# Patch embedding of a vision tower: seven of eight block products for seven pairs of chunks

## The chip, the cores and the metric

The kernel runs on one core of a Trainium2 chip. The metric is the device time of one execution in microseconds (us). Three runs of the kernel before took 1721.77, 1724.46 and 1727.43 us, so its median is 1724.46 us. One further execution was taken by the hardware profiler, and all rows below come from it.

## The reference

128 images of 3 x 224 x 224 fp32 pass through a patch embedding and two transformer layers (attention, a routed MLP, attention, a mixture of two of eight experts). Only the first step is touched by the change:

```
patches = X.reshape(B, 3, 8, 28, 8, 28).transpose(0, 2, 4, 1, 3, 5).reshape(B, 64, 2352)
tokens  = einsum('bpi,hi->bph', patches, W) + b          # 2352 -> 128
tokens  = concatenate([class_token, tokens], axis=1) * pos_embed
```

It is one matrix product: 128 outputs, a contraction over 2352 = 18 x 128 + 48 inputs, and 128 x 64 = 8192 patches as columns, all in fp32.

## The kernel before, in words

The program is a chain of stages, each a block in which the five engines run their own instruction lists and meet at its end. `patch_embed` (L100) is the first; `layer_norm`, `attention` and the rest follow and read `h`, the tokens that `patch_embed` writes.

The patches are cut into 16 chunks of 8 images, that is 512 columns each. The host lays a chunk out as 18 slices of 128 inputs (`x_main`, 4.6 MB a chunk) and a rest of 48 inputs (`x_tail`). The buffer `xb` holds two whole chunks of 18 slices.

- SyncE (`block.sync`) issues all loads of x on one queue. Chunk c is loaded in six transfers of 768 KB (three slices each, L168) once chunk c-2 has been used; for the first chunk each is preceded by the three weight slices of the same place (L167). The rests of two chunks follow (L181), one in partitions 0 to 47 and one in 64 to 111 of `xe`.
- TensorE (`block.tensor`) takes two chunks at a time. For each it accumulates 18 matmuls of a 128x128 weight slice with a 128x512 slice of x in one PSUM bank (L201). Then come the two matmuls of the rests (L209), with 64 rows each. An fp32 matmul appears in the trace as two MATMUL records and two LDWEIGHTS records.
- VectorE adds the bias, multiplies by the position embedding and writes `h` (L228), one instruction a chunk.
- ScalarE waits for the fourth chunk and then loads the constants of the later stages (L131); GpSimd prepares a few small constants from them. Both are nearly idle in this stage.

The loops are written with `pipelined`, which puts the middle of the work into a hardware loop. The stage ends for the others when TensorE's last product is done and VectorE has written the last two chunks; the next stage's first matmul (L329) needs that.

The functions below are those that the diff touches, with what calls them.

Of the kernel before, what the change touches and what calls it, by code (L numbers as in the profile page):

```python
# [14 lines left out]
ALU = mybir.AluOpType  # L15
ACT = mybir.ActivationFunctionType
# [26 lines left out]
class At:  # L43


    def __init__(self, index, slot):
        self.index, self.slot = index, slot


def pipelined(eng, items, unroll, depth, lag, step):  # L50

    groups, lead = items // unroll, -(-(depth + lag) // unroll)
    assert lead < groups

    def group(g, fixed):
        for j in range(unroll):
            def at(s, j=j):  # L60
                slot = (j - s) % unroll
                if fixed:
                    i = g * unroll + j - s
                    return At(i, slot) if 0 <= i < items else None
                return At(g * unroll + (j - s), slot)
            step(j, at)

    for g in range(lead):
        group(g, True)
    with eng.Fori(lead, groups) as g:  # L70
        group(g, False)
    for g in range(groups, -(-(items + depth) // unroll)):
        group(g, True)


# [24 lines left out]
def patch_embed(nc, images, x_main, x_tail, h, ps, w_src, w_tok, b_tok, pos, cls, own_loads, later_loads, consts):  # L100

    n = CHUNK_IMAGES * PATCHES
    chunks = images // CHUNK_IMAGES
    pieces = 6
    kp = KT // pieces
    half = P // 2
    ctx, sb, sem = stage_scope(nc)  # L110
    with ctx:  # L111
        xb = sb("x_chunk", [P, 2, KT, n])
        xe = sb("x_ends", [P, 2, n])
        x_in = [[sem(f"x_in_{s}_{i}") for i in range(pieces)] for s in range(2)]
        end_in = [sem(f"x_end_in_{s}") for s in range(2)]
        w_in = [sem(f"w_in_{i}") for i in range(pieces)]
        w_end_in, ends_clear = sem("w_end_in"), sem("ends_clear")
        x_used, tok_ps = sem("x_used"), sem("tok_ps")
        tok_done, cls_done = sem("tok_done"), sem("cls_done")
        own_loaded, later_loaded = sem("own_loaded"), sem("later_loaded")  # L120
        means_set, gelu_done, asum_done, folded = sem("means_set"), sem("alphas_gelu"), sem("alpha_summed"), sem("folded")
        block = ctx.enter_context(nc.Block())

        @block.scalar
        def _(act):
            for dst, src in own_loads:
                act.dma_start(dst, src).then_inc(own_loaded, 16)
            act.wait_ge(own_loaded, 16 * len(own_loads))
            act.wait_ge(tok_ps, 4)
            for dst, src in later_loads:  # L130
                act.dma_start(dst, src).then_inc(later_loaded, 16)  # L131
            act.wait_ge(later_loaded, 16 * len(later_loads))
            nc.scalar.activation(consts.alphas[:, :, :], consts.alpha_raw, ACT.Gelu).then_inc(gelu_done, 1)
            act.wait_ge(gelu_done, 1)

        @block.gpsimd
        def _(pool):
            nc.gpsimd.memset(consts.mean_w[:, :], 1.0 / D).then_inc(means_set, 1)
            nc.gpsimd.memset(consts.spread_w[:, :], 1.0 / 32).then_inc(folded, 1)
            nc.gpsimd.memset(consts.dist_pair[:, :, :], 0.0).then_inc(folded, 1)  # L140
            pool.wait_ge(means_set, 1)
            pool.wait_ge(later_loaded, 16 * len(later_loads))
            nc.gpsimd.tensor_tensor(consts.center_w[:, :], consts.ident[:, :], consts.mean_w[:, :], ALU.subtract)\
                .then_inc(folded, 1)
            nc.gpsimd.tensor_scalar(consts.neg_b_q[:, :], consts.b_q, -1.0, None, ALU.mult).then_inc(folded, 1)
            pool.wait_ge(gelu_done, 1)
            nc.gpsimd.tensor_tensor(consts.asum[:, :], consts.alphas[:, :, 0], consts.alphas[:, :, 1], ALU.add)\
                .then_inc(asum_done, 1)
            pool.wait_ge(asum_done, 1)
            nc.gpsimd.tensor_tensor(consts.asum[:, :], consts.asum[:, :], consts.alphas[:, :, 2], ALU.add)\  # L150
                .then_inc(asum_done, 1)
            pool.wait_ge(asum_done, 2)
            nc.gpsimd.tensor_tensor(consts.abv[:, :], consts.asum[:, :], consts.bv_col, ALU.mult).then_inc(folded, 1)
            pool.wait_ge(folded, 5)

        @block.sync
        def _(sp):
            def step(j, at):
                a = at(0)
                s = a.slot % 2  # L160
                fixed = isinstance(a.index, int)
                if not (fixed and a.index < 2):
                    sp.wait_ge(x_used, a.index - 1)
                for i in range(pieces):
                    ks = slice(i * kp, (i + 1) * kp)
                    if fixed and a.index == 0:
                        sp.dma_start(w_tok[:, ks, :], w_src[:, ks, :]).then_inc(w_in[i], 16)  # L167
# [19 lines left out]
        def _(pe):  # L187
            def step(j, at):
# [3 lines left out]
                if not (fixed and a.index < 2):  # L192
                    pe.wait_ge(tok_done, a.index * 2 - 2)
# [2285 lines left out]
```

## Time and profile before

| | us |
|---|---|
| median of three runs | 1724.46 |
| lowest, highest | 1721.77, 1727.43 |
| span of the profiled execution | 1699.7 |
| first matmul of the patch embedding | 6.47 |
| its last matmul record begins and lasts | 265.39, 1.13 for the last four |
| first matmul of the next stage | 268.45 |
| TensorE busy over the whole span | 1616.2 (95%) |
| VectorE, ScalarE, GpSimd busy | 1082.2, 869.2, 782.4 |

The span runs from the first to the last instruction; the runs are timed around the whole execution, which adds some 25 us. PE is TensorE, PEld its weight loads, DVE is VectorE, ACT is ScalarE, POOL is GpSimd, SP is SyncE; a q behind the name is the engine's sequencer or queue. A row of the lines view gives source line, engine, operation, output <- inputs, shapes, count, then busy time and mean ns of one, then the idle time of the engine ahead of the group and what ended it. A row of the windows view gives, for one stretch of time, its length and each engine's busy time with the number of instructions, then the granted TensorE clock, the share of time the DMA engines were busy and what they moved in GB/s. The patch embedding is the first 268 us of the span.

### The profile page before, as it was taken

How to read it: one execution, taken by the hardware profiler on the slowest of the kernel's cores; microseconds unless marked ns; L12 is line 12 of the kernel's file. 1: busy time of each engine (PE TensorE's matmuls, PEld its weight loads, DVE VectorE, ACT ScalarE, POOL GpSimd, SP SyncE). 2: the span in 40 equal slices, each digit the busy share in tenths (PEclk: the TensorE clock that was granted, in tenths of full speed). 3: DMA queues.
4: the chain of work that ended last, by engine and by line, in shares of the span. 5: the costliest groups of instructions: out<-in, count | busy, mean ns of one | idle time of the engine just before them, and what ended most of it. 6: DMA issues, size and time to landing. Idle time of an engine off the chain costs nothing. (4 is left out here: it accounts for less than half of the span.)

```text
span 1699.7 us, 61682 instructions
## 1 busy us (share of the span) xinstructions
PE 1616.2 (95%) x24097; PEld 1203.3 (71%) x24097; DVE 1082.2 (64%) x3361; ACT 869.2 (51%) x2334; POOL 782.4 (46%) x932
## 2 busy tenths in 40 slices
PE   8999999899999999997989998999999999869997
PEld 3444444677877777776567755888888888659997
DVE  0000005688888888885676664577777777768875
ACT  0000004666666666663544445566766666547753
POOL 0000000588888888886001111445555555645554
PEclk9999999999999999999989999999999999969999
DMA  9887860000000000000400000000000000135431
GB/s 366 338 309 301 321 244 1 2 4 4 3 3 3 3 3 3 3 3 4 111 1 1 1 1 5 3 8 22 22 21 21 21 24 18 36 102 154 141 80 44
DMA packets 47214, 117.17 MB, mean 69 GB/s; under 512 B 10731, under 2 KB 29470, under 8 KB 46972
## 3 DMA queue, kind: packets, MB, share of 16 engines
q1 hardware_dynamic: 39198, 99.25, 16.4%
q0 software_dynamic: 6096, 12.94, 2.2%
q8 instruction: 191, 3.13, 0.8%
q10 hardware_dynamic: 1678, 1.43, 0.3%
q14 instruction: 51, 0.42, 0.1%
HBM read 96.80 MB, written 18.61 MB: 68 GB/s over the span
## 5 line engine op out<-in xcount | busy, mean ns | idle before, releaser
L1545 PE MATMUL ps<-xn,s_a_wqkv 128*128 128x260 f32 x1024 | 276.9, 402 | 4.5 <-DMA s_a_wqkv<-in_f_b 2.9
L201 PE MATMUL ps<-x_chunk,s_w_tok 128*128 128x512 f32 x576 | 252.1, 599 | 6.5 <-DMA x_chunk<-in_x_main 6.5
L201 PEld LDWEIGHTS ps<-x_chunk,s_w_tok 128*128 128x128 f32 x576 | 109.9, 192 | 147.4 <-issue 147.4
L1545 PEld LDWEIGHTS ps<-xn,s_a_wqkv 128*128 128x128 f32 x1024 | 177.0, 191 | 50.2 <-issue 16.3
L228 DVE SCALAR_TENSOR_TENSOR h<-ps,s_b_tok,s_pos 128x512 f32 (+1 forms) x16 | 11.3, 746 | 248.8 <-PE ps L209 248.8
L886 POOL TENSOR_TENSOR prob_a<-e_a,inv_sum_a 128x512 f32<-128x512 f32 x64 | 66.9, 1045 | 194.4 <-issue 113.4
L2161 POOL DMA_INDIRECT out<-h,xn x93 | 97.6, 1049 | 89.6 <-DVE h L2276 85.1
L1629 PE MATMUL ps<-s_a_wqkv,xn_pair_a 128*64 128x256 f32 x1024 | 138.8, 391 | 0.0
L941 ACT ACTIVATE resT_a<-ps 128x260 f32<-128x260 f32 x256 | 85.2, 386 | 101.4 <-PE ps L1596 64.6
L1411 DVE TENSOR_REDUCE neg_max_a<-ps 128x8 f32<-128x520 f32 x128 | 89.2, 697 | 70.8 <-PE ps L1519 48.5
L870 POOL TENSOR_TENSOR kept_a<-e_a,keep_a 128x585 f32<-128x585 f32 x64 | 87.2, 1362 | 71.0 <-issue 60.4
L1596 PE MATMUL ps<-probT_a,horner_a 64*64 64x65 f32 x2048 | 113.6, 228 | 4.2 <-issue 2.6
L771 POOL MEMSET cls_queries_a<- 128x1040 f32 x2 | 1.9, 966 | 238.1 <-POOLq L283 238.1
L1586 PE MATMUL ps<-dv_a,probT_a 64*64 64x64 f32 x2048 | 107.0, 223 | 2.8 <-DVE probT_a L1170 2.3
L1586 PE MATMUL ps<-horner_a,probT_a 64*64 64x64 f32 x2048 | 105.7, 220 | 0.6 <-issue 0.6
L929 ACT ACTIVATE qk_a<-ps 128x260 f32<-128x260 f32 x256 | 96.4, 387 | 18.7 <-PE ps L1545 11.8
L1586 PEld LDWEIGHTS ps<-dv_a,probT_a 64*64 64x64 f32 x2048 | 82.3, 136 | 27.5 <-issue 27.4
L2051 POOL TENSOR_TENSOR h<-h,mlp_gated 128x320 f32<-128x320 f32 x26 | 22.4, 860 | 167.8 <-DVE mlp_gated L2031 167.8
L394 ACT ACT_TABLE_LOAD x3 | 3.8, 1283 | 184.1 <-PEq L111 176.8
L1596 PE MATMUL ps<-probT_a,cls_values_a 64*64 64x1 f32 x2048 | 91.6, 187 | 3.3 <-issue 3.2
L1420 DVE TENSOR_TENSOR e_a<-ps,neg_max_a 128x520 f32<-128x520 f32 x128 | 89.7, 701 | 6.0
L1106 ACT ACTIVATE e_a<-e_a 128x585 f32<-128x585 f32 (+1 forms) x128 | 85.3, 666 | 14.7 <-DVE e_a L1420 7.7
(280 smaller groups left out, 4265.6 us busy)
## 6 DMA issues: line engine op xcount, KB each, us to landing
x_chunk<-in_x_main SPq DMA_DIRECT2D x96, 768.0 KB, 8.8
xn<-pair_rows SPq DMA_DIRECT2D x93, 130.0 KB, 2.1
pair_rows<-pad_rows_m SPq DMA_DIRECT2D x29, 130.0 KB
s_f_all<-in_f_w SPq DMA_DIRECT2D x2, 1024.0 KB
x_ends<-in_x_tail SPq DMA_DIRECT2D x16, 96.0 KB, 10.8
out<-h,xn POOLq DMA_INDIRECT x93
s_w_tok<-in_w_tok SPq DMA_DIRECT2D x6, 192.0 KB, 8.2
pair_rows<-rows_m,slot_i_m POOLq DMA_INDIRECT x65, 2.5
```

The source lines that it names most:

```text
L201: last = nc.tensor.matmul(ps[:, bank, :], w_tok[:, k, :], xb[:, s, k, :], start=(k == 0), stop=False)
L870: nc.gpsimd.tensor_tensor(columns(kept, t.even), columns(e_of(t), t.even), columns(keep, t.even), ALU.mult).then_inc(kept_done, 1)
L929: nc.scalar.activation(qk[:, (t.j // 2) % 2, c, :], ps[:, QK_BANK[i], 0:QUAD], ACT.Identity if bias is not None else ACT.Copy, bias=bias[: ...
L941: nc.scalar.activation(res_t[:, k // 2, :, at[0], at[1], :], ps[:, R_BANK[i], 0:CH * SEQ].rearrange("p (c q) -> p c q", q=SEQ), ACT.Copy). ...
L1106: nc.scalar.activation(columns(e_of(t), t.even), columns(e_of(t), t.even), ACT.Exp, scale=-SCALE)\
L1411: last = nc.vector.tensor_reduce(neg_max[:, :, 0:CH], score(), AX.X, ALU.min)
L1420: last = nc.vector.tensor_tensor(e_of(t)[:, :, 0:CH], score(), over_keys(neg_max[:, :, 0:CH]), ALU.subtract)
L1545: nc.tensor.matmul(ps[:, QK_BANK[i], 0:QUAD], w_qkv[:, c * P:(c + 1) * P], xn[:, t.h * QUAD:(t.h + 1) * QUAD], start=True, stop=True).then ...
L1586: last = nc.tensor.matmul(ps[rows, 2 + n, col:col + DH], pt[rows, k, c, i, 1:SEQ], values[rows, i, c, :], start=True, stop=True)
L1596: last = nc.tensor.matmul(ps[other, R_BANK[i], c * SEQ:c * SEQ + cols], values[rows, (t.j - 6) % 2, i, c, :], pt[rows, k, c, i, 0:cols], s ...
L1629: last = nc.tensor.matmul(ps[b * DH:(b + 1) * DH, V_BANK, i * CH * DH:(i + 1) * CH * DH] .rearrange("p (c d) -> p c d", c=CH), xs[:, k, i ...
L2161: nc.gpsimd.indirect_dma_start(self.out[:, :], bass.IndirectOffsetOnAxis(ap=blk[:, s % RB, self.NAME:self.NAME + 1].bitcast(mybir.dt.int32 ...
```

## The change

The chunks are taken in eight pairs and the 18 slices as nine pairs (slice k with slice k+9; HK = 9). In a step k the four 64-column halves of the two weight slices and the four x slices (two chunks, two slices) form a 2 x 2 block product. Before, it took four 128-column matmuls, which are eight products of a 64-column half. Strassen's method (in Winograd's form) does it with seven, from sums and differences of the blocks, and adds the seven results up afterwards. Seven pairs of chunks (63 steps) are done this way and the eighth the former way.

- TensorE does seven matmuls a step with 64 weight columns, each writing one half (partitions 0 to 63, `lo`, or 64 to 127, `hi`) of one of four PSUM banks. The order within a step begins with `lo` in even steps and with `hi` in odd ones, so that the halves alternate over the whole stream. Pairs of chunks alternate between banks 0 to 3 and 4 to 7.
- VectorE computes for each step three differences of 128x512 slices (`tr[.., 0]`, `[.., 1]`, `[.., 3]`), staggered over three iterations: iteration j makes term 0 of step j, term 1 of step j-1 and term 3 of step j-2. GpSimd computes the fourth difference (`tr[.., 2]`). The ring `tr` has four places and lies in `xn`, which is free in this stage.
- VectorE also forms the five weight sums, once for each three slices.
- After nine steps ScalarE copies the four banks to SBUF with eight instructions (`evict`), GpSimd adds parts with five instructions (`join` at its k = 5), VectorE adds two more and finishes the two chunks (`join` at its k = 8).
- x is loaded in sets of three steps (12 transfers of 256 KB for the first set, one step at a time; 4 transfers of 768 KB for a later one) into three buffers; set s waits for the steps of set s-3. The tail of the second chunk is loaded once more (`xd`), and GpSimd makes a difference of the tails.
- ScalarE loads the constants of the later stages behind its first eviction. The hardware loops of the stage are gone: all is unrolled.

The core of the diff (the removed code is printed above):

```diff
+    folded = pairs - 1
+    HK = KT // 2
+    TRI = 3
+    SETS = HK // TRI
+    steps = folded * HK
+    RT = 4
...
+        xb = sb("x_chunk", [P, SETS, 4, TRI, n])
+        sums = sb("w_sums", [P, 5, HK, half])
+        tr = xn[:, 0:RT * 4 * n].rearrange("p (r q n) -> p r q n", r=RT, q=4)
...
+            for s in range(pairs * SETS):                                   # SyncE
+                p, i = divmod(s, SETS)
+                if s < SETS:
+                    load_w(i)
+                    load_w(SETS + i)
+                since(sp, step_done, TRI * (s - SETS + 1))
+                for kk in range(TRI if s == 0 else 1):
+                    for q in range(4):
+                        c, k = 2 * p + q % 2, (q // 2) * HK + i * TRI
+                        if s == 0:
+                            load(xb[:, 0, q, kk:kk + 1, :], c, k + kk, 1).then_inc(first_in[kk], 16)
+                        else:
+                            load(xb[:, i, q, :, :], c, k, TRI).then_inc(x_in[i], 16)
...
+                t = tr[:, m % RT]                                           # TensorE, step m
+                sides = ((0, lo), (1, hi)) if low_first else ((1, hi), (0, lo))
+                for i, side in sides:
+                    product(0, side, w_tok[:, (HK + k, k)[i], lo], x_at(m, (2, 0)[i]))
+                pe.wait_ge(t_done[0], m + 1)
+                pe.wait_ge(t_done[1], m + 1)
+                for i, side in sides:
+                    product(2, side, sums[:, i, k, :], t[:, i])
+                pe.wait_ge(t_done[3], m + 1)
+                for i, side in sides:
+                    product(1, side, sums[:, 3 + i, k, :], (x_at(m, 3), t[:, 3])[i])
+                pe.wait_ge(t_done[2], m + 1)
+                product(3, lo if low_first else hi, sums[:, 2, k, :], t[:, 2], start=k < 2, stop=k >= HK - 2)\
+                    .then_inc(step_done, 1)
...
+            def third_term(m):                                              # GpSimd
+                x_ready(pool, m)
+                since(pool, step_done, m - RT + 1)
+                nc.gpsimd.tensor_tensor(tr[:, m % RT, 2], x_at(m, 3), x_at(m, 1), ALU.subtract)\
+                    .then_inc(t_done[2], 1)
...
+            for j in range(steps + 2):                                      # VectorE
+                if j < steps:
+                    if j < HK and j % TRI == 0:
+                        weight_sums(j // TRI)
+                    x_ready(dve, j)
+                    since(dve, step_done, j - RT + 1)
+                    nc.vector.tensor_tensor(tr[:, j % RT, 0], x_at(j, 1), x_at(j, 0), ALU.subtract)
+                if 1 <= j <= steps:
+                    dve.wait_ge(t_done[0], j)
+                    nc.vector.tensor_tensor(tr[:, (j - 1) % RT, 1], x_at(j - 1, 3), tr[:, (j - 1) % RT, 0], ...)
+                if j >= 2:
+                    dve.wait_ge(t_done[1], j - 1)
+                    nc.vector.tensor_tensor(tr[:, (j - 2) % RT, 3], tr[:, (j - 2) % RT, 1], x_at(j - 2, 2), ...)
+                p, k = divmod(j, HK)
+                if k == 8 and p and j < steps:
+                    join(p - 1)
+            join(folded - 1)
```

## Rows read from the trace of the kernel before

**Rows 1.** Windows of the patch embedding, and of the start of the next stage.
```profile
0.00:10.00 10.00, 3.53 (x4) 1.51 (x5) 1.25 (x2) 0.00 (x0) 0.70 (x7) 1.00 0.72 244
10.00:30.00 20.00, 20.00 (x46) 8.89 (x45) 0.00 (x0) 0.00 (x0) 0.00 (x0) 1.00 1.03 396
100.00:200.00 100.00, 100.00 (x237) 43.22 (x236) 4.23 (x6) 0.00 (x0) 0.00 (x0) 1.00 0.77 301
270.00:300.00 30.00, 27.86 (x219) 13.26 (x217) 21.97 (x33) 16.07 (x30) 0.53 (x1) 1.00 0.01 2
```

**Rows 2.** Lines of 0 to 255 us: who waits in the stage.
```profile
L201 PE MATMUL ps<-x_chunk,s_w_tok 128*128 128x512 f32 x552 | 241.8, 599 | 6.5 <-DMA x_chunk<-in_x_main 6.5
L228 DVE SCALAR_TENSOR_TENSOR h<-ps,s_b_tok,s_pos 128x512 f32 x10 | 7.0, 746 | 153.9 <-PE ps L209 153.9
```

**Rows 3.** Timeline of TensorE: start us, us, engine line, what, how many records.
```profile
6.47 6.00 PE L201 MATMUL ps<-x_chunk,s_w_tok 128*128 128x512 f32 x7 [6.47 <-DMA x_chunk<-in_x_main]
...
40.30 1.13 PE L209 MATMUL ps<-x_ends,s_w_tok 64*128 64x512 f32 x4
41.36 8.85 PE L201 MATMUL ps<-x_chunk,s_w_tok 128*128 128x512 f32 x20
...
265.39 1.13 PE L209 MATMUL ps<-x_ends,s_w_tok 64*128 64x512 f32 x4
266.72 1.41 DVE L228 SCALAR_TENSOR_TENSOR h<-ps,s_b_tok,s_pos 128x512 f32 x2 [30.75 <-PE ps L209]
```

**Rows 4.** Timeline of TensorE in attention, full width and half width.
```profile
699.71 2.20 PE L1545 MATMUL ps<-xn,s_a_wqkv 128*128 128x260 f32 x8
704.66 1.08 PE L1629 MATMUL ps<-s_a_wqkv,xn_pair_a 128*64 128x256 f32 x8
```

**Rows 5.** Timeline: a VectorE stream beside a GpSimd instruction, one input in PSUM.
```profile
700.62 1.28 DVE L1157 TENSOR_TENSOR horner_a<-ps,v_alpha_a 128x512 f32<-128x512 f32 x2
700.83 1.43 POOL L870 TENSOR_TENSOR kept_a<-e_a,keep_a 128x585 f32<-128x585 f32 x1 [1.33 <-issue]
```

**Rows 6.** One source line of VectorE each: count, ns min/median/max; its two inputs are in SBUF.
```profile
L1306 DVE TENSOR_TENSOR weight_of_choice_m<-each_choice_m,choice_weights_m x16: 224/1061/1120, 1115.5 to 1491.9; 128x64 f32<-128x64 f32 x15, 128x80 f32<-128x80 f32 x1
```

**Rows 7.** Timeline around one of them.
```profile
1252.10 0.22 DVE L1300 TENSOR_TENSOR each_choice_m<-s_expert_ids,index_m 128x64 f32<-128x64 f32 x1
1252.35 1.12 DVE L1306 TENSOR_TENSOR weight_of_choice_m<-each_choice_m,choice_weights_m 128x64 f32<-128x64 f32 x1
...
1252.34 1.04 POOL L886 TENSOR_TENSOR prob_a<-e_a,inv_sum_a 128x512 f32<-128x512 f32 x1 [3.62 <-DVE inv_sum_a L1455]
```

**Rows 8.** One source line each: ns min/median/max of the nearest GpSimd, VectorE, ScalarE instructions.
```profile
L855 POOL TENSOR_TENSOR cls_values_a<-dv_a,horner_a x64: 1261/1272/1281, 329.0 to 797.3; 128x512 f32<-128x512 f32 x64
L886 POOL TENSOR_TENSOR prob_a<-kept_a,inv_sum_a x64: 1040/1042/1047, 313.6 to 786.2; 128x512 f32<-128x512 f32 x64
L1157 DVE TENSOR_TENSOR horner_a<-ps,v_alpha_a x128: 678/680/692, 324.6 to 800.2; 128x512 f32<-128x512 f32 x128
L1993 DVE TENSOR_TENSOR first_choice<-s_expert_ids,index_r x13: 491/493/494, 861.7 to 983.9; 128x320 f32<-128x320 f32 x13
L966 ACT ACTIVATE v_raw_a<-ps x64: 597/598/605, 307.9 to 781.5; 128x512 f32<-128x512 f32 x64
```

**Rows 9.** Windows with the granted clock behind stretches of little TensorE work.
```profile
310.00:315.00 5.00, 1.71 (x40) 1.04 (x40) 3.32 (x9) 3.23 (x11) 2.83 (x4) 1.00 0.00 0
315.00:320.00 5.00, 4.86 (x48) 3.86 (x48) 2.87 (x11) 3.21 (x9) 4.47 (x5) 0.66 0.00 0
325.00:330.00 5.00, 4.18 (x108) 3.40 (x108) 3.94 (x13) 3.04 (x9) 4.83 (x6) 1.00 0.01 3
```

**Rows 10.** DMA issues of the stage: KB each, median us from issue to landing.
```profile
x_chunk<-in_x_main SPq DMA_DIRECT2D x96, 768.0 KB, 8.8
```

More of the change, by code:

```diff
@@ L40 @@
 ROW = 2 * D + 4
[L43 to L73, printed above, removed]
 spent = []
@@ L134, in _ @@
             act.wait_ge(gelu_done, 1)
+            for p in range(2, folded):
+                evict(p)
         @block.gpsimd
         def _(pool):
-            nc.gpsimd.memset(consts.mean_w[:, :], 1.0 / D).then_inc(means_set, 1)
[L139 to L142, printed above, removed]
@@ L186, in _ @@
-        @block.tensor
-        def _(pe):
-            def step(j, at):
-                a = at(0)
-                fixed = isinstance(a.index, int)
-                first = fixed and a.index == 0
-                if not (fixed and a.index < 2):
-                    pe.wait_ge(tok_done, a.index * 2 - 2)
-                for s in range(2):
-                    bank = 2 * a.slot + s
-                    for i in range(pieces):
-                        if first and s == 0:
-                            pe.wait_ge(w_in[i], 16)
-                        pe.wait_ge(x_in[s][i], a.index * 16 + 16)
-                        for k in range(i * kp, (i + 1) * kp):
-                            last = nc.tensor.matmul(ps[:, bank, :], w_tok[:, k, :], xb[:, s, k, :],
-                                                    start=(k == 0), stop=False)
-                    last.then_inc(x_used, 1)
-                if first:
-                    pe.wait_ge(w_end_in, 32)
-                pe.wait_ge(end_in[a.slot], (a.index - a.slot) * 16 + 32)
-                for s in range(2):
-                    rows = slice(s * half, (s + 1) * half)
-                    nc.tensor.matmul(ps[:, 2 * a.slot + s, :], w_tok[rows, KT, :], xe[rows, a.slot, :],
-                                     start=False, stop=True).then_inc(tok_ps, 1)
-            pipelined(pe, chunks // 2, 2, 0, 2, step)
@@ new lines, in _ @@
+            nc.gpsimd.memset(consts.mean_w[:, :], 1.0 / D).then_inc(means_set, 1)
+            nc.gpsimd.memset(consts.spread_w[:, :], 1.0 / 32).then_inc(folded_w, 1)
+            nc.gpsimd.memset(consts.dist_pair[:, :, :], 0.0).then_inc(folded_w, 1)
+            for m in range(steps):
+                p, k = divmod(m, HK)
+                third_term(m)
+                if k == 1:
+                    ends_gap(p)
+                if k == 5 and p:
+                    join(p - 1, m)
+                if p == 3 and k == 2:
+                    fold_constants()
@@ L213, in _ @@
+            join(folded - 1, steps - 1)
+            pool.wait_ge(folded_w, 5)
         @block.vector
@@ L236 @@
+            join(folded - 1)
+            for c in range(2):
+                dve.wait_ge(tok_ps, c + 1)
+                finish(2 * folded + c, ps[:, 4 * (folded % 2) + c, :])
 class Router:
```

240 lines of the change are left out of this document (173 added, 67 removed).

## Prediction

> **What bounds the kernel now.** I read the windows of the first stage first. TensorE is busy for every microsecond from 6.47 us on, at full clock, while the DMA share falls to 0.77 in mid-stage [rows 1]: the loads have room, and in the lines no matmul waits for one after the first [rows 2]. VectorE has one instruction a chunk and waits for TensorE, GpSimd and ScalarE have next to nothing. So TensorE's stream sets the length: it runs from 6.47 to 266.5 us, and VectorE's last two instructions follow [rows 3]. In the timeline 20 records take 8.85 us [rows 3]; less the 0.16 us by which a record (0.59 us) outlasts the pace, that is 0.43 us a record, 0.86 us a matmul. 288 matmuls are 248 us; the rests of a pair of chunks add about 1.26 us (1.06 from start to start and two slower changes, eight times, 10 us), and the first records run at half pace (7 in 6.0 us), 2 us more. That is the 260 us seen. All later stages start from `h` and are not touched.
>
> **What TensorE saves.** A step is 8 half-width products before (4 matmuls, 8 records, 3.44 us) and 7 after. This only helps if two half-width products run at once. Attention shows it: 8 records of 128x64 weights on 256 columns, alternating between the two halves, take 1.08 us, while 8 full-width records of 260 columns take 2.20 us one after the other [rows 4]. So the pair costs what one costs, and since the halves alternate across steps the odd seventh product pairs with the first of the next step. A step costs 3.5 x 0.86 = 3.01 us, 63 steps save 63 x 0.43 = 27 us. The rests (now four 64x64 products, one on each quarter) I leave at 1.26 us. The last lone half and the change of width before the last pair give back 0.5 us. TensorE alone would so save 26.6 us.
>
> **What feeds it.** Each step now needs three VectorE differences and one GpSimd difference of 128x512, and a pair of chunks needs in addition on GpSimd five joining sums and one of the tails, on VectorE two sums and two finishing instructions: 31 VectorE and 15 GpSimd instructions in a pair, nearly all with both inputs in SBUF. VectorE's nearest rows are 0.68 us for one with an input in PSUM, two in 1.28 us, so 0.60 us from start to start [rows 5, 8]; 320 columns with both in SBUF take 0.49 us, on the same line of 0.16 us plus one element per 1.04 ns [rows 8]. GpSimd's are 1.27 us with two full inputs and 1.04 us with one broadcast [rows 8]. Taken each by itself: VectorE 31 x 0.60 = 18.6 us, GpSimd 15 x 1.27 = 19 us, TensorE 9 x 3.01 + 1.26 = 28.35 us. Both would hide.
>
> They do not run by themselves. L1306, a VectorE product of 64 columns with both inputs in SBUF, should take 0.22 us as its neighbour L1300 does, and its median is 1.06 us [rows 6, 7]. In the timeline GpSimd's 1.04 us instruction starts at 1252.34 and the VectorE one at 1252.35; it ends 0.09 us after GpSimd's end [rows 7]. It stood still for the whole of it. L1157, with one input in PSUM, runs beside GpSimd at its normal pace [rows 5]. So two-input SBUF work on the two engines adds up instead of overlapping. The Trainium skill, "SBUF — State Buffer", section "Who interferes with whom", says the same as a rule: a VectorE instruction with two SBUF inputs and a GpSimd instruction that reads SBUF exclude each other, and whichever comes second waits until the first is finished. By that rule the change's two streams are one; a rule of free overlap would give the saving above.
>
> The price of a pair of chunks, as one stream: of 31 VectorE instructions 15 follow a GpSimd one; such a one has its start-up hidden (L1306 ends 0.09 us behind, not 0.22), so 0.55 us, the other 16 take 0.60: 17.9 us. 15 GpSimd instructions at 1.23 us (1.27 less a little overlap from start to start): 18.5 us. Together 36.3 us against TensorE's 28.35, so this stream becomes the bound. Its two ends: 31 x 0.55 + 15 x 1.04 = 32.7 us if GpSimd holds VectorE off only for the shorter of its two times, and 31 x 0.69 + 15 x 1.27 = 40.4 us if nothing of a start-up is hidden. I take 36.3, which uses the rows of the same shape. ScalarE's eight copies (0.60 us each, 4.8 us a pair) [rows 8] lie beside all this: the join starts on GpSimd only two steps later.
>
> **The start.** VectorE's iteration j first waits for the x of step j, and then makes the last term of step j-2. So TensorE cannot finish step 1 before the x of step 3 is there, which is set 1, a semaphore that wants all 3.15 MB. Through set 1 the queue moves 0.39 + 3.15 + 0.35 (rests) + 0.39 + 3.15 = 7.4 MB. At 2.44 MB by 10 us and 396 GB/s behind [rows 1] this is 22.6 us, plus 1 us to be signalled, and I add 2 for the first set's short 2 KB rows: 25.5 us (23 to 28). Set 2 follows 3.54 MB, 8.6 us, later at 34. Before, TensorE had been running since 6.47 us.
> From 25.5 us the shared stream goes on: iterations 3 to 8 are 6 x (3 x 0.60 + 1.23) = 18.2 us, the last weight sums some 1.8 us (five of 192 columns at 0.35, an estimate between the 0.22 of 64 columns and 0.49 of 320 [rows 7, 8]), the tail difference 1.2 us: 46.7 us. Set 2 is not late for this (wanted at about 36). Six more pairs, each with the join of the one before: 6 x 36.3 = 218 us, to 264.5. Two iterations and the end of step 62 add 3.5: 268. Then the classic pair, 72 x 0.43 + 0.1 + 1.26 = 32.3 us, beside which the last join (some 14 us) hides: TensorE ends at 300.3 us, where it ended at 266.5. VectorE's two final instructions are the same. The sum is +34 us.
>
> Loads in the steady state: a set of 3.15 MB takes some 2 us to start and 7.9 us to move at 396 GB/s (a single transfer lands in 8.8 us at the median, in a full queue [rows 10]); a pair of 36 us needs three, so they are no bound. SyncE's wait for a used set holds back only the sets and tails behind it. What stands behind VectorE's waits is every later difference, in order; that is why one late set or one GpSimd instruction reaches TensorE. The later stages' constants (1.4 MB, now earlier) fit as well. The stage's sequencers get more instructions; I charge nothing, since attention issues more per microsecond.
>
> **Forecast.** Against the profiled execution's own time the span goes from 1699.7 to about 1734 us; the runs' median lies 24.8 us above that span, for what is around it, so 1724.5 + 34 = 1758 us. With the two ends of the pair's price (6 x -3.6 and 6 x +4.1 us, pair 0 with them by -2 to +3) and of the start (2.5 us either way) this case spans 1732 to 1788.
>
> **Rivals.**
> (1) No exclusion that matters: the engines' long instructions interleave after all, or GpSimd's are blocked for only a small part. Then TensorE binds. Step 1's last term comes at 25.5 + 1.9 = 27.4; the rest of step 1 and step 2 at half pace, after the long idle time, end at 33.5; six steps and the rests 19.3: pair 0 done at 52.8. Six pairs at 28.35 are 170, the lone half and change 0.5, the classic pair 32.2: 255.6 us, 11 less than 266.5; with 2 us lost once to the constants' transfer, -9: 1715 us. For it: each engine's own busy sum fits. Against it: with a median of 1.06 us at least half of L1306's 16 instances were held off. The time turns from a loss to a gain when a pair costs less than about 31 us.
> (2) TensorE's clock falls. With 28 us of work in 36 it stands still for about 1 us in a step. Behind 1.71 us of work in 5 us the granted clock was 0.66 in the next window, but with 4.18 of 5 it stayed at 1.00 [rows 9]. If it ran at 1.2 GHz throughout, a step would take 6.0 us and 54 steps about 108 us more than the 4.0 of the forecast: 1865 us. Gaps of 1 us speak against it.
> (3) The halves don't pair at 512 columns, so that the change does not do what it says: 7 x 0.86 = 6.0 us a step, 63 x 2.6 = 162 us more, about 1890 us with the start. Rows 4 speak against it; I know of no row at 512 columns.
>
> **How the numbers follow.** The forecast 0.77, rival 1 0.14, rival 2 0.06, rival 3 0.03. 0.3% (5 us) is about what a measurement of this kernel tells from no change. Rival 1's spread reaches into that band, as does the lowest end of the forecast's: faster 0.12, within 0.05, slower 0.83. The range 1722 to 1792 leaves out most of rival 1 and all of rivals 2 and 3.
>
> **What would show it.** In the new profile VectorE's differences with a mean well over 0.69 us, near 1.1, or GpSimd's over 1.27; in a mid-stage window the two engines' own work summing to the whole time while TensorE is at some 75%; TensorE idle before the third to sixth product of a step and released by VectorE's terms; a pair period of 36 us. If the periods are 28 us and the differences 0.69 us, the exclusion is what I had wrong. The start is right if step 1 waits until about 27 us. The half-width products should show 7 in 3.0 us where nothing waits.

## The result, and the profile after

| | before | after |
|---|---|---|
| median of four runs, us | 1724.99 | 1769.51 |
| lowest, highest | 1721.77, 1727.43 | 1768.43, 1771.34 |
| span of the profiled execution | 1699.7 | 1768.1 |
| first matmul of the next stage | 268.45 | 307.32 |
| VectorE, GpSimd busy over the span | 1082.2, 782.4 | 1310.9, 951.3 |

The change makes the kernel slower by 44.5 us: ratio 1.026, with the 95% interval 1.0244 to 1.0276. The forecast was 1758, its range 1722 to 1792. The patch embedding itself ends 38.9 us later, where +34 was forecast.

The profiled spans differ by 68.4 us, which is more than the runs show. The one profiled execution of before was a short one: in a second one of the same kernel (e5 below) the span is 1725.1 us, the next stage starts at 268.39 us, as before, and 17 of the 25.4 us between the two lie in the second attention stage, which the change doesn't touch. So medians are compared with medians here, and of the profiled executions only the stage.

Windows of the kernel after, as in [rows 1]: stretch, its length, then busy time and count of TensorE, its weight loads, VectorE, ScalarE and GpSimd, then granted clock, DMA share, GB/s.

```profile
0.00:10.00 10.00, 0.88 (x2) 0.29 (x4) 4.03 (x8) 0.00 (x0) 1.54 (x8) 1.00 0.79 244
10.00:30.00 20.00, 9.94 (x24) 2.32 (x22) 12.02 (x14) 0.00 (x0) 9.23 (x6) 0.92 1.04 382
24.00:34.00 10.00, 4.46 (x13) 1.39 (x14) 6.50 (x8) 0.00 (x0) 4.07 (x3) 0.66 0.85 345
...
100.00:200.00 100.00, 83.66 (x356) 24.70 (x354) 96.14 (x84) 9.51 (x16) 69.74 (x47) 0.97 0.72 271
...
260.00:300.00 40.00, 38.53 (x116) 15.47 (x113) 11.58 (x16) 4.75 (x8) 8.58 (x7) 1.00 0.44 163
```

In the hundred microseconds in which TensorE had been busy throughout [rows 1] it is now busy for 83.66. VectorE shows 96.14 for 84 instructions and GpSimd 69.74 for 47. Together that is more than 100, because a blocked instruction counts as busy on its own engine while the other one works. The DMA share is 0.72: the loads have room.

The lines of 0 to 320 us show the same from the waiter's side. Columns as in [rows 2].

```profile
L167 PE MATMUL ps<-xn,w_sums 128*64 128x512 f32 x504 | 194.6, 622 | 26.5 <-DVE xn L351 23.3 <-DVE xn L347 3.2
L249 POOL TENSOR_TENSOR xn<-x_chunk 128x512 f32<-128x512 f32 x63 | 102.6, 1638 | 90.3 <-PE ps L167 72.3 <-DMA x_chunk<-in_x_main 17.5
...
L347 DVE TENSOR_TENSOR xn<-x_chunk,xn 128x512 f32<-128x512 f32 x63 | 82.2, 1305 | 0.0
L343 DVE TENSOR_TENSOR xn<-x_chunk 128x512 f32<-128x512 f32 x63 | 72.3, 1147 | 23.2 <-DMA x_chunk<-in_x_main 12.7 <-PE ps L167 10.0
...
L351 DVE TENSOR_TENSOR xn<-xn,x_chunk 128x512 f32<-128x512 f32 x63 | 66.9, 1063 | 0.0
```

VectorE's three differences take 1.31, 1.15 and 1.06 us in the mean, where a free one takes 0.68; TensorE's idle time ends on two of them. The same three, and GpSimd's difference, by source line: ns min/median/max.

```profile
L343 DVE TENSOR_TENSOR xn<-x_chunk x63: 677/693/1797, 9.1 to 262.7; 128x512 f32<-128x512 f32 x63
...
L347 DVE TENSOR_TENSOR xn<-x_chunk,xn x63: 677/1750/1805, 12.4 to 267.1; 128x512 f32<-128x512 f32 x63
...
L249 POOL TENSOR_TENSOR xn<-x_chunk x63: 1283/1729/1876, 9.2 to 260.5; 128x512 f32<-128x512 f32 x63
```

There are two kinds of each and little between them: a VectorE instruction takes 0.68 us when it is free and about 1.75 when it comes second, and GpSimd's takes 1.28 or about 1.73. In the timeline one can see them stand on each other (start us, duration us, engine, line):

```profile
156.72 1.71 POOL L254 TENSOR_TENSOR x_ends_gap<-x_ends,x_ends_gap 64x512 f32<-64x512 f32 x1
...
157.23 1.75 DVE L343 TENSOR_TENSOR xn<-x_chunk 128x512 f32<-128x512 f32 x1
158.90 0.68 DVE L347 TENSOR_TENSOR xn<-x_chunk,xn 128x512 f32<-128x512 f32 x1
159.50 0.68 DVE L351 TENSOR_TENSOR xn<-xn,x_chunk 128x512 f32<-128x512 f32 x1
...
160.24 1.11 PE L167 MATMUL ps<-x_chunk,w_sums 128*64 128x512 f32 x1 [3.21 <-DVE xn L351]
```

GpSimd's tail difference runs to 158.43. VectorE's L343, begun at 157.23, ends 0.55 us behind it; the next two, with GpSimd idle, take 0.68. TensorE stands for 3.21 us until the third of them. Its first records behind such a gap take 1.11 us instead of 0.59: the granted clock is 0.66 in the window of 24 to 34 us, which mixes the levels of 1.2 and 2.4 GHz, and 0.50, the lower level throughout, from 29.6 to 33.0 us, right behind the first gap.

### The profile page after: what moved, and what is told of

Its sections match the earlier page's. It is cut to its first block and busy times, and to the rows that moved or that the text cites. A ratio compares the mean times of both kernels' runs of the same rounds, so it can differ in the third digit from the quotient of the medians.

```text
span 1768.1 us, 62873 instructions
## 1 busy us (share of the span) xinstructions
PE 1630.3 (92%) x24503; PEld 1183.1 (67%) x24503; DVE 1310.9 (74%) x3580; ACT 904.1 (51%) x2391; POOL 951.3 (54%) x1037
## 5 line engine op out<-in xcount | busy, mean ns | idle before, releaser
L167 PE MATMUL ps<-xn,w_sums 128*64 128x512 f32 x504 | 194.6, 622 | 26.5 <-DVE xn L351 23.3
L249 POOL TENSOR_TENSOR xn<-x_chunk 128x512 f32<-128x512 f32 x63 | 102.6, 1638 | 90.3 <-PE ps L167 72.3
L167 PEld LDWEIGHTS ps<-xn,w_sums 128*64 128x64 f32 x504 | 56.1, 142 | 111.1 <-issue 73.1
L167 PE MATMUL ps<-x_chunk,s_w_tok 128*64 128x512 f32 x252 | 99.9, 625 | 9.1 <-DMA x_chunk<-in_x_main 9.1
L1649 PE MATMUL ps<-qk_a 64*64 64x65 f32 x4096 | 95.8, 225 | 12.0 <-issue 10.8
L1649 PEld LDWEIGHTS ps<-qk_a 64*64 64x64 f32 x4096 | 76.2, 134 | 41.2 <-issue 34.3
L229 ACT ACTIVATE part_a<-ps 128x512 f32<-128x512 f32 x7 | 4.2, 598 | 183.5 <-PE ps L167 183.5
```

Source lines behind the costliest of these rows:

```text
L167: return nc.tensor.matmul(ps[side, base + bank, :], weights, moving, start=k == 0 if start is None else start, stop=k == HK - 1 if stop is ...
L249: nc.gpsimd.tensor_tensor(tr[:, m % RT, 2], x_at(m, 3), x_at(m, 1), ALU.subtract)\
L1649: last = nc.tensor.matmul(ps[i * PATCHES:(i + 1) * PATCHES, b, c * SEQ:(c + 1) * SEQ], qk[rows, sl, c, t0 + 1:t0 + SEQ], qk[rows, sl, CH + ...
```

## The experiments

**e1: the two engines side by side, measured alone.** The kernel before with spare 128x512 instructions at the start of VectorE and GpSimd, in six phases, while TensorE does its usual work.

```diff
+            for phase, behind in enumerate((10, 10, 17, 24, 31)):
+                pool.wait_ge(m_pool, 2 + 5 * phase)
+                pool.wait_ge(m_dve, behind)
+                for r in range(5):
+                    if phase == 3:
+                        nc.gpsimd.memset(u[11 + r], 0.5).then_inc(m_pool, 1)
+                    else:
+                        nc.gpsimd.tensor_tensor(u[11 + r], u[9], u[10], ALU.add).then_inc(m_pool, 1)
...
+            for phase, behind in enumerate((2, 7, 12, 17, 22)):
...
+                for r in range(7):
+                    if phase == 4:
+                        last = nc.vector.tensor_copy(u[2 + r], u[0])
+                    elif phase == 2:
+                        last = nc.vector.tensor_tensor(u[2 + r], ps[:, 6, :], u[1], ALU.add)
+                    else:
+                        last = nc.vector.tensor_tensor(u[2 + r], u[0], u[1], ALU.add)
```

> The kernel before, with 35 VectorE and 25 GpSimd instructions of 128x512 fp32 on spare data added to the patch embedding, where both engines are idle. Phases of 7 and 5: VectorE alone; GpSimd alone; both with two SBUF inputs; VectorE with one input in PSUM beside GpSimd with two in SBUF; VectorE with two SBUF inputs beside a GpSimd memset; a VectorE copy beside GpSimd with two SBUF inputs. Exclusion theory: alone 0.60 us from start to start and 1.27 us; together the phase lasts as long as the sum, 7 x 0.6 + 5 x 1.2 = 10.2 us; with a PSUM input and beside the memset both run as alone (the longer of 4.2 and 6.3 us). Rival, that the two only share bandwidth or that VectorE was slowed by TensorE and the loads: together about 6.5 us, or VectorE already slow when alone.

Windows of e1, one for each phase: VectorE alone; GpSimd alone; both with two SBUF inputs; VectorE with one input in PSUM beside GpSimd; VectorE beside GpSimd's memset; VectorE's copy (one input) beside GpSimd.

```profile
7.83:12.13 4.30, 4.30 (x8) 1.75 (x7) 4.30 (x7) 0.00 (x0) 0.00 (x0) 1.00 1.02 416
12.29:18.48 6.19, 6.19 (x15) 2.66 (x14) 0.00 (x0) 0.00 (x0) 6.14 (x5) 1.00 1.02 407
18.53:28.21 9.68, 9.68 (x24) 4.33 (x23) 9.68 (x7) 0.00 (x0) 7.93 (x5) 1.00 1.03 377
28.25:34.55 6.30, 6.30 (x16) 2.84 (x15) 4.27 (x7) 0.00 (x0) 6.19 (x5) 1.00 1.02 417
34.61:38.95 4.34, 4.34 (x11) 1.90 (x10) 4.30 (x7) 0.00 (x0) 2.38 (x5) 1.00 1.01 415
38.99:46.78 7.79, 7.79 (x20) 3.07 (x19) 7.79 (x7) 0.00 (x0) 7.06 (x5) 1.00 1.03 366
```

Seven VectorE instructions alone take 4.30 us (0.614 each), five of GpSimd 6.19 (1.238 each). Side by side they take 9.68, where full overlap would give 6.19 and a plain sum 10.49. With one VectorE input in PSUM both run as if alone (4.27 and 6.19), and beside a memset too (4.30). So whether the two exclude each other goes by where the inputs lie, and nothing of it comes from this stage's waits: TensorE is busy throughout at full clock in all six phases, and the one run took 1724.76 us. The Trainium skill, "SBUF — State Buffer", section "Who interferes with whom", states these cases as a rule, the harmless write-only GpSimd instruction among them; all phases agree with it.

**e2: the change, with GpSimd reading nothing in its difference.** A memset of the same tile stands in its place, so the fourth difference is left out of the result.

```diff
-                nc.gpsimd.tensor_tensor(tr[:, m % RT, 2], x_at(m, 3), x_at(m, 1), ALU.subtract)\
-                    .then_inc(t_done[2], 1)
+                nc.gpsimd.memset(tr[:, m % RT, 2], 0.5).then_inc(t_done[2], 1)
```

> The changed kernel, with GpSimd's difference of each step replaced by a memset of the same tile (that term is left out of the result). Exclusion theory: GpSimd reads SBUF only in six instructions a pair, 31 x 0.60 + 6 x 1.23 = 26 us, under TensorE's 28.4; the pair falls from 35.9 to about 28.7 us, 6 x 7.2 = 43 us and some 4 us of the first pair: near 1723 us. Rival, that VectorE is slowed by TensorE's streams or by the loads: the pair stays at 35 to 36 us and half of VectorE's differences at 1.75 us.

1725.02 us against 1723.10, ratio 1.0013 (0.9991 to 1.0035); the next stage starts at 267.57 and a pair of chunks takes (217.0 - 36.6) / 6 = 30.1 us. Lines of e2, 0 to 300 us:

```profile
L350 DVE TENSOR_TENSOR xn<-xn,x_chunk 128x512 f32<-128x512 f32 x63 | 57.9, 921 | 0.0
...
L346 DVE TENSOR_TENSOR xn<-x_chunk,xn 128x512 f32<-128x512 f32 x63 | 51.6, 819 | 0.0
...
L249 POOL MEMSET xn<- 128x512 f32 x63 | 32.5, 525 | 118.2 <-PE ps L167 67.7 <-DMA x_chunk<-in_x_main 50.1
```

With one instruction of GpSimd a step no longer reading SBUF, +1.9 us is left of +44.5, though the waits, semaphores and transfers are the same. The instruction is also 0.7 us shorter, and e2 alone doesn't tell which of the two counts: if the memset still excluded VectorE, a pair would be 31 x 0.614 + 6 x 1.238 + 9 x 0.53 = 31.2 us, near the 30.1 measured; e1's fifth phase tells it. GpSimd's six other instructions a pair still block, as the means of 0.92 and 0.82 us show. They were in my expectation of 28.7 us, though, and don't explain the 1.4 us over it. Most of that lies in the second pair: from VectorE's first difference (L342) of this pair to that of the next it is 35.3 us, 4.8 of them VectorE's waits for x, and from then on 29.1, 28.6, 29.9 and 29.7 us.

**e3: the joining sums moved from GpSimd to VectorE,** spread over five iterations.

```diff
-                if k == 5 and p:
-                    join(p - 1, m)
...
+                if part == 0:
+                    dve.wait_ge(evicted, 8 * (p + 1))
+                    add(part_d[hi, 0, :], part_d[hi, 0, :], part_d[hi, 1, :])
+                    add(swap_c[:, :], swap_c[:, :], part_c[:, :])
```

> The changed kernel, with the five joining sums of a pair moved from GpSimd to VectorE and spread over its iterations; GpSimd keeps the fourth difference and that of the tails. Exclusion theory: 36 x 0.60 + 10 x 1.2 = 33.6 us a pair instead of 35.9, so 6 x 2.3 = 14 us less than the changed kernel, near 1756 us. Rival, that each engine is slow by itself: VectorE has five more instructions at its present mean of 1.17 us, 6 us a pair more, near 1800 us.

1749.15 against 1723.10, ratio 1.0153 (1.0128 to 1.0178); pair (240.4 - 38.4) / 6 = 33.7 us; next stage at 293.16, 14.2 us earlier than after the change, where 14 was expected. The median less its own before fell by 18.5.

**e4: GpSimd's whole share on VectorE.** Added to e3: the fourth difference and that of the tails.

```diff
-                third_term(m)
...
+                if 1 <= j <= steps:
+                    nc.vector.tensor_tensor(tr[:, (j - 1) % RT, 2], x_at(j - 1, 3), x_at(j - 1, 1),
+                                            ALU.subtract).then_inc(t_done[2], 1)
```

> The changed kernel with everything on VectorE: four differences a step, the tails' difference and the joining sums; GpSimd has nothing to do but the small constants. Exclusion theory: 46 x 0.60 = 27.6 us a pair, just under TensorE's 28.4; the pair takes 28.5 to 30 us, some 40 us less than the changed kernel, 1722 to 1738 us. Rival, that VectorE's instructions are slow by themselves here: 46 x 1.17 = 54 us a pair, about 110 us more than the changed kernel.

1722.61 against 1723.10, ratio 0.9998 (0.9981 to 1.0016); pair (214.0 - 36.9) / 6 = 29.5 us; next stage at 265.13. Lines of e4, 0 to 300 us:

```profile
L340 DVE TENSOR_TENSOR xn<-x_chunk 128x512 f32<-128x512 f32 x63 | 43.2, 686 | 22.8 <-DMA x_chunk<-in_x_main 19.0 <-PE ps L167 3.6
...
L344 DVE TENSOR_TENSOR xn<-x_chunk,xn 128x512 f32<-128x512 f32 x63 | 43.0, 683 | 0.0
```

This is the opposite of what one does by busy sums: 46 instructions on one engine are faster by 6.4 us a pair than 31 and 15 on two. A GpSimd instruction costs the shared stream 1.24 us, the same work on VectorE 0.61. The window of e4, 100 to 200 us, has both engines near full:

```profile
100.00:200.00 100.00, 99.95 (x463) 41.98 (x461) 98.61 (x160) 14.28 (x24) 0.00 (x0) 1.00 0.88 335
```

**e5: the kernel before, once more,** unchanged, to see whether its first profiled span was ordinary.

> The kernel before, unchanged, profiled once more. Its first profiled execution had a span of 1699.7 us, while its timed runs are 1719 to 1729 us; for the changed kernel time and span differ by 1.7 us only. If the first profiled execution was a fast outlier in the second attention loop (570 us from the first to the last of its value projections, against 586 in every other profile so far), this one shows a span near 1721 us, the patch embedding ending again at 268.4 us and the loop at 586. If the profiler really leaves out 25 us for this kernel, the span is again 1700.

One run of 1726.87 us, with a span of 1725.1: what lies around the span is 1.8 us and not 24.8. The next stage starts where it did. The row of a source line of attention, count and ns as above, then first and last start:

```profile
L1629 PE MATMUL ps<-s_a_wqkv,xn_pair_a x1024: 379/379/431, 306.7 to 1483.2; 128*64 128x256 f32 x171
```

**e6: e4 with a start by single steps.** The first nine steps of x are loaded and awaited one by one instead of by threes, and in each iteration the terms whose data are there come ahead of the one that waits.

```diff
-                for kk in range(TRI if s == 0 else 1):
+                for kk in range(TRI if s < SETS else 1):
...
+                if j < steps:
+                    if j < HK and j % TRI == 0:
+                        weight_sums(j // TRI)
+                    x_ready(dve, j)
```

> Everything on VectorE, and in addition the first nine steps' x loaded and signalled step by step, and within an iteration the third difference ahead of the wait for the next x. Theory: the shared stream being gone, what is left of the loss is the late start (step 1 waits for all of set 1 at 25.5 us); with it cured step 3 ends near 24 instead of 36 us, and the stage about 12 us earlier: 1706 to 1714 us, below the kernel before. Rival, that the start does not matter because VectorE's 46 instructions a pair bind afterwards: within 3 us of the version with the old start, 1720 to 1726 us.

1711.68 against 1722.34, ratio 0.9936 (0.9911 to 0.9961); first rests at 26.4 (e4: 36.9), pair 29.6, next stage at 254.55, 10.6 us earlier than in e4, where some 12 was expected. It is faster than both kernels.

**e7: the start alone.** The change with the loads by single steps, the order of the terms and GpSimd's share as they were.

```diff
-        first_in = [sem(f"x_first_{i}") for i in range(TRI)]
+        first_in = [sem(f"x_first_{i}") for i in range(HK)]
...
-                for kk in range(TRI if s == 0 else 1):
+                for kk in range(TRI if s < SETS else 1):
```

> The changed kernel with only the loads and signals of the first nine steps made step by step; GpSimd keeps its work and VectorE its order. Exclusion theory: the shared stream of 36 us a pair binds from the third step on, but it can begin some 8 us earlier, so up to 8 us less than the changed kernel, 1761 to 1768 us. Rival, that the slow start is the larger part of the loss: 20 us or more are won.

1758.60 against 1722.34, ratio 1.0209 (1.0179 to 1.0240), a little under the 1761 to 1768 that I expected. That the time is near is luck: of up to 8 us expected in this stage it gained 0.65, since the next stage starts at 306.67. Step 3 of pair 0, behind which the first rests stand, is done 7.9 us earlier (31.5 against 39.4), pair 0 itself only 4.1 us (the first eviction begins at 53.45 against 57.59). The timeline of e7 shows the first place where the gain goes: VectorE wants set 3 at 39.5 us and it isn't there yet, while the change comes to it at 48.35 and doesn't wait.

```profile
43.05 0.69 DVE L343 TENSOR_TENSOR xn<-x_chunk 128x512 f32<-128x512 f32 x1 [3.52 <-DMA x_chunk<-in_x_main]
43.09 3.45 POOL L249 TENSOR_TENSOR xn<-x_chunk 128x512 f32<-128x512 f32 x2 [4.97 <-DMA x_chunk<-in_x_main]
```

VectorE's first final sum (L328), once a pair, starts at 76.80, 114.18, 151.60, 189.04, 226.46 and 263.90 in e7 and at 80.88, 116.53, 152.47, 189.71, 227.09 and 264.55 after the change. So 4.1 us are left at the first join, and e7's pairs then take 37.4 us throughout, while the change's took 35.7 and 35.9 before they took 37.2 to 37.5. The windows of the change's first and third of these periods show what the short ones lack:

```profile
80.88:116.53 35.65, 31.48 (x142) 9.57 (x140) 35.28 (x32) 6.25 (x10) 24.17 (x15) 1.00 0.73 276
...
152.47:189.71 37.24, 31.84 (x136) 9.47 (x134) 35.38 (x33) 4.75 (x8) 24.04 (x15) 0.95 0.70 262
```

The granted clock is 1.00 in the change's two short periods and 0.95 in its three long ones and in all five of e7. In the long ones TensorE stands for 3.2 us behind the join, its next records run at half pace, and VectorE's first difference of a later step then waits for TensorE to free a place of the ring: 1.77, 1.93 and 1.98 us, at 163.75, 201.15 and 238.59. In the short ones its waits for TensorE are 0.3 us and 1.2 us in all. So at the joins the low clock does reach the shared stream, by some 1.6 us a pair (an estimate, 37.4 less 35.8). No run here changes the clock alone, and a gap of 3.2 us in the second short period left it at 1.00, so why it falls in one pair and not in the other stays open. That the timed median is 11 us under the change's, with its own reference 2.7 lower, is mostly outside this stage.

**e8: the fourth difference on VectorE, the joins left on GpSimd.** Other half of e4, as e3 is the first.

```diff
-                third_term(m)
...
+                    nc.vector.tensor_tensor(tr[:, (j - 1) % RT, 2], x_at(j - 1, 3), x_at(j - 1, 1),
+                                            ALU.subtract).then_inc(t_done[2], 1)
```

> The changed kernel with the fourth difference moved to VectorE, the joining sums and the tails' difference left on GpSimd. Exclusion theory: 40 x 0.60 + 6 x 1.2 = 31.2 us a pair instead of 35.9, about 28 us for six pairs and some 3 of the first: near 1738 us. It should lie between the version with all on VectorE (1722.6) and that with the joining sums there (1749.2). Rival, that each engine is slow by itself: nine more VectorE instructions of 1.17 us a pair, slower than the changed kernel.

1734.27 against 1722.34, ratio 1.0074 (1.0050 to 1.0099); pair (224.0 - 36.2) / 6 = 31.3 us, where 31.2 was expected; next stage at 274.61.

With e1's prices the four divisions of the same work can be set beside each other; the plain sum is 0.614 us for each VectorE and 1.238 for each GpSimd instruction of a pair:

| | VectorE, GpSimd instructions | plain sum | measured pair | next stage | median less its own before |
|---|---|---|---|---|---|
| the change | 31, 15 | 37.6 | 35.9 | 307.32 | +44.5 |
| e3 | 36, 10 | 34.5 | 33.7 | 293.16 | +26.1 |
| e8 | 40, 6 | 32.0 | 31.3 | 274.61 | +11.9 |
| e4 | 46, 0 | 28.2 | 29.5 | 265.13 | -0.5 |

The measured pair is the mean from the first rests to those of the seventh pair. It follows the plain sum, less 0.7 to 1.7 us, as long as GpSimd has part of it; e4's mean holds waits for x up to 87 us, and its last four periods of L340 are 29.7, 28.6, 29.3 and 28.7 us. By work that overlaps, GpSimd's 18.6 us a pair (15 x 1.238) and VectorE's 19.0 (31 x 0.614) would have hidden behind TensorE, and the change would have run at TensorE's own pace.

**e9: e6 with the later stages' constants loaded after the sixth eviction,** to take their 1.4 MB out of the crowded queue of the start.

```diff
-            evict(0)
+            for p in range(folded - 1):
+                evict(p)
             for dst, src in later_loads:
                 act.dma_start(dst, src).then_inc(later_loaded, 16)
-            evict(1)
+            evict(folded - 1)
```

> The version with everything on VectorE and the stepwise start, in addition with the loads of the later stages' constants (1.4 MB) moved from behind the first eviction to behind the sixth, where the queue of x has room. If these loads hold back x in the second pair, the stage ends up to 3.5 us earlier (1.4 MB at 0.4 MB per us). If not, nothing changes: TensorE's long wait in that version is at 41 to 47 us, before they are issued at 52, so I expect no more than 1 us and 1710 to 1713 us.

1713.76 against 1727.70, ratio 0.9922 (0.9903 to 0.9942); next stage at 254.10 against e6's 254.55. Nothing to speak of, as expected.

**e10: e9 with twelve steps by single loads** in place of nine. In e6 TensorE waits at 41 to 47 us for set 3, which its semaphore reports as a whole.

```diff
-                for kk in range(TRI if s < SETS else 1):
+                for kk in range(TRI if s <= SETS else 1):
```

> The same, and the x of the tenth to twelfth step (set 3) also signalled step by step. Theory: the wait at 41 to 47 us is for a semaphore that wants the whole set 3, with the load queue full since the start; step by step TensorE can begin step 9 some 5 us earlier and does not fall to half pace behind the gap, so the stage ends 4 to 6 us earlier than in the version before it: 1704 to 1708 us. Rival: the queue's bytes bind anyway, and TensorE only waits in three places instead of one: less than 2 us.

1711.38 against 1727.70, ratio 0.9902 (0.9883 to 0.9920); next stage at 254.25. My theory, that the wait was for the whole set where one step of it was already there, fell: I expected 4 to 6 us and the stage got none. Windows of e6 and then of e10:

```profile
40.00:44.00 4.00, 1.36 (x8) 0.20 (x4) 0.63 (x2) 0.00 (x0) 0.00 (x0) 0.99 1.04 290
44.00:48.00 4.00, 3.28 (x8) 1.01 (x10) 4.00 (x8) 0.00 (x0) 0.00 (x0) 0.50 0.99 406
```

```profile
40.00:44.00 4.00, 4.00 (x22) 1.43 (x20) 2.57 (x5) 0.76 (x1) 0.00 (x0) 1.00 1.07 297
48.00:60.00 12.00, 8.45 (x32) 2.68 (x30) 7.44 (x12) 1.41 (x3) 0.00 (x0) 0.86 0.95 378
```

The gap at 40 us is closed, and a gap of the same size opens at 48 to 60 us, with the DMA share at 0.95. Up to there the queue's bytes bind, and no order of waiting helps. e6, e9 and e10 can't be told apart by their intervals; all three beat the kernel before by 0.6 to 1.0%.

## Why the prediction was right, step by step

**The exclusion, and the price of a pair.** I had put the pair at 36.3 us, as one stream of VectorE and GpSimd. The four products of the rests (L195) run once a pair, behind step 3 in the first pair, from 39.4 us, and in the seventh, from 254.6 (the row ends with its last record): 35.9 us in the mean. These six intervals hold VectorE's join only five times. From VectorE's first difference of the second pair, at 48.35 us, to the instruction behind its join in the seventh, at 267.08, all six joins are in, and a pair is 36.5 us.

```profile
L195 PE MATMUL ps<-x_ends,s_w_tok x42: 589/615/909, 39.4 to 255.1; 64*64 64x512 f32 x42
```

e1 shows the exclusion by itself, e2 that without the reading GpSimd instruction the loss is gone, e3, e8 and e4 that the loss shrinks with GpSimd's share. Rival 1 (overlap, 1715) had what e1's fourth and fifth phases show as its condition, and the seven pairs have neither a VectorE input in PSUM nor a large write-only GpSimd instruction. The working behind 36.3 was less good than its result, and that part is luck. It had 1.35 us a pair of overlap; e1's seven and five together save 0.81 us of 10.49, which for 15 GpSimd instructions would be 2.4 us and a pair of 35.2 (an estimate from e1). The pair began at 35.7 and then settled at 37.4, with VectorE's wait for TensorE behind the low clock (e7 above), a term that the forecast put at nothing. The two errors nearly cancel in the mean.

**TensorE's part.** The halves do pair at 512 columns; rival 3 is out. Where nothing waits, the timeline of the kernel after has one record of each half at the same time, 0.43 us from one pair of them to the next:

```profile
270.66 0.59 PE L167 MATMUL ps<-xn,w_sums 128*64 128x512 f32 x1
...
271.08 0.59 PE L167 MATMUL ps<-x_chunk,s_w_tok 128*64 128x512 f32 x1
271.09 1.01 PE L167 MATMUL ps<-xn,w_sums 128*64 128x512 f32 x2
...
273.33 2.84 PE L212 MATMUL ps<-x_chunk,s_w_tok 128*128 128x512 f32 x6
```

Fourteen records a step at that pace are the 3.0 us forecast. A whole pair comes down to nearly my 28.35 us once GpSimd is out of it and x is there in time. The means of 29.5 and 29.6 in e4 and e6 hold waits for x, in e6 the gap at 41 to 47 us. From 96.49 us on, e6's first final sums follow each other at 28.52 us, four times; from there to 210.57 TensorE is busy for 114.05 of 114.08 us and VectorE for 113.33. No matmul is recorded as waiting for VectorE there, nor VectorE for TensorE, though some weight loads wait for it. With 46 VectorE instructions at 0.614 being 28.2 us the two are nearly balanced, and which one sets the last tenths is open.

**The start.** Set 1 was there at 25.46 us, where I had 25.5. The bytes in the queue gave 22.6 of it; the other 3 us, for the signal and the short rows, were estimates that no row before had shown, and no run here takes them apart. Timeline of the kernel after:

```profile
25.46 0.69 DVE L343 TENSOR_TENSOR xn<-x_chunk 128x512 f32<-128x512 f32 x1 [4.30 <-DMA x_chunk<-in_x_main]
25.50 3.49 POOL L249 TENSOR_TENSOR xn<-x_chunk 128x512 f32<-128x512 f32 x2 [5.48 <-DMA x_chunk<-in_x_main]
26.07 1.77 DVE L347 TENSOR_TENSOR xn<-x_chunk,xn 128x512 f32<-128x512 f32 x1
27.76 1.78 DVE L351 TENSOR_TENSOR xn<-xn,x_chunk 128x512 f32<-128x512 f32 x1
...
29.60 1.12 PE L167 MATMUL ps<-xn,w_sums 128*64 128x512 f32 x1 [5.54 <-DVE xn L351]
```

I had named 27 us as the sign for the release of step 1; it came at 29.6, because both of VectorE's next terms stand behind GpSimd's two: 27.4 was the value without exclusion, and I didn't carry my own main point into this line. It is carried on in part. TensorE's records run at half pace behind that gap, and at 33.4 us VectorE has waited 2.04 us and GpSimd 4.43 us for it to free a place. With that and the class token's instruction (1.38 us, left out of the sum) the second pair begins at 48.35, where I had 46.7. That the start was worth working out is shown by e6 against e4: 10.6 us of stage for the order of loads and terms, where e7 shows that the loads alone are worth 0.65 us while the shared stream binds.

**The end of the stream, the term that was too small.** I had the classic pair start at 268; it starts at 273.33. I had the last join in the stream done at 264.5, and it is done at 267.08: 1.6 us of that come from the first pair and 1 us from the six others. The join stands in iteration 62, ahead of the terms that steps 61 and 62 still need:

```profile
266.42 0.74 DVE L321 SCALAR_TENSOR_TENSOR h<-swap_c,s_b_tok,s_pos 128x512 f32<-128x512 f32 x1
267.08 0.68 DVE L347 TENSOR_TENSOR xn<-x_chunk,xn 128x512 f32<-128x512 f32 x1
267.68 1.28 DVE L351 TENSOR_TENSOR xn<-xn,x_chunk 128x512 f32<-128x512 f32 x2
```

VectorE is through at 268.96, and TensorE needs 4.4 us more, about a step and a half at 3.0 us, where I had given the end of a step. From the join to the classic pair it is 6.25 us instead of 3.5. From 273.33 to the next stage are 34.0 us, as forecast (32.3 and two instructions of VectorE). These two parts, 2.6 and 2.7 us, are the 5 us by which the stage missed: +38.9 instead of +34.

**The clock, rival 2.** I said that gaps of 1 us a step speak against it. The gaps are not of 1 us. Waits of the stage after (who, count, longest in us):

```profile
PE ps L167 <- DVE xn L351: 36.7, 24, 5.5
```

24 gaps of 1.5 us in the mean, up to 5.5, and behind some of the long ones the clock is granted at the lower level for a few records (0.50 from 29.6 to 33.0 us). The rival's price of 108 us needed that level throughout, which didn't come: over 100 to 200 us the clock is 0.97. But it was not free. VectorE's waits for TensorE behind the records at half pace come to 7.7 us (2.04, 1.77, 1.93 and 1.98), so a few of the 38.9 us are the clock's, as far as these waits show it.

**What lies around the span.** "The runs' median lies 24.8 us above that span, for what is around it" was wrong as a reason: e5 puts that at 1.8 us, and the rest was one short execution. The sum was made as a difference, so the error didn't reach the forecast; had I worked from the span after, 1768.1 + 24.8, it would have.

**What stays open.** Of the 44.5 us, 38.9 are in this stage. The other 5.6 lie behind it, in stages with the same instructions; the forecast had nothing there, and with the 5 us of the stage they make up most of the 11.5 us between 1758 and 1769.51. The difference between a kernel's timed change and its stage's change is +5.6 for the change, +1.3 for e3, +5.8 for e8, +2.8 for e2 and e4, +3.2 for e6, +0.4 for e9, -2.1 for e10 and -2.0 for e7. So it wanders by a few microseconds in both directions, and I found no cause for it.

## What to carry to other kernels

Before work is divided between VectorE and GpSimd, look where its inputs lie: with two inputs in SBUF on the one and an SBUF read on the other, the two came out nearly as one engine here (9.68 us of a plain sum of 10.49), and GpSimd is the one that costs twice as much for the same 128x512 instruction (1.238 against 0.614 us). Look in the profile for a VectorE line whose median is far over its minimum while GpSimd works; one such line of 64 columns [rows 6] was enough to forecast a stage here. Where the waits leave TensorE idle for some microseconds, count in what its records at half pace hand back to the engines that wait for it, here some 1.6 us a pair by the estimate above. And an algorithm that saves an eighth of TensorE's work has to be paid in elementwise instructions on the engine beside it: this one paid off only after all of them had gone to VectorE and the start had been ordered by the bytes of the queue.

## What I had not expected of the hardware

- A VectorE copy of fp32 with a single SBUF input is excluded as well. Its shortest in e1 is 0.41 us, which I take for its time alone, though no phase has it alone; beside GpSimd seven take 7.79 us, 1.11 each, and most of them 1.48. The Trainium skill, "SBUF — State Buffer", section "Who interferes with whom", gives this for copies in their two-port mode; e1's sixth phase agrees. Moving an add to a copy is no way out.
- GpSimd is held up too, though less: its differences take 1.73 us at the median where a free one takes 1.28.
- A GpSimd memset of 128x512 takes 0.53 us (e2) and didn't hold VectorE up: in e1 VectorE's seven took 4.30 us beside five of them, as alone.
- The second attention loop of the kernel before, untouched by any of this, took some 17 us less in one profiled execution than in the other: its last value product starts at 1465.5 us in the first profile and at 1483.2 in the second, with the same instructions. A span of a single profile is no measure of a change of one per cent.
